# Softmax shifts of one column each, and an addition of zeros for the copy of the bias columns

## What is computed

```python
def _cross_attention(q_in, kv_in, wq, bq, wk, bk, wv, bv, wo, bo, bias_k, bias_v):
    qh = (q_in @ wq + bq).reshape(b, q_len, H, K)
    kh = (kv_in @ wk + bk).reshape(b, t, H, K)
    vh = (kv_in @ wv + bv).reshape(b, t, H, K)
    kh = jnp.concatenate([kh, jnp.broadcast_to(bias_k, (b, 1, H, K))], axis=1)
    vh = jnp.concatenate([vh, jnp.broadcast_to(bias_v, (b, 1, H, K))], axis=1)
    logits = jnp.einsum('bqhk,bthk->bhqt', qh, kh) / scale
    weights = jax.nn.softmax(logits, axis=-1)
    ctx = jnp.einsum('bhqt,bthk->bqhk', weights, vh).reshape(b, q_len, H * K)
    return ctx @ wo + bo
...
x = res + _cross_attention(_layer_norm(x, ...), xf, ...)     # twice
h = jax.nn.gelu(_layer_norm(x, ...) @ w_fc1 + b_fc1, approximate=False) @ w_fc2 + b_fc2
return x + h
```

## Time and profile before

| | |
|---|---|
| median of 3 runs | 567.76 us (566.6 to 568.83) |
| span of the profiled execution | 565.1 us |
| PE busy | 548.0 us (97%) |
| PEld busy | 492.8 us (87%) |
| DVE busy | 408.8 us (72%) |
| ACT busy | 315.1 us (56%) |
| POOL busy | 330.1 us (58%) |
| chain that ended last | PE 82%, DVE 11%, issue 3%, DMA 1%, ACT 1% |

### The profile page before, as it was taken

One profiled execution on the slowest core, in us unless ns is written; L12 is line 12 of the kernel. 1 busy time (PEld: TensorE's weight loads), 2 busy tenths in 40 slices (PEclk: granted clock), 3 DMA queues, 4 the chain that ended last, 5 costly groups with the idle time before them and its releaser, 6 DMA issues.

```text
span 565.1 us, 11067 instructions
## 1 busy us (share of the span) xinstructions
PE 548.0 (97%) x3665; PEld 492.8 (87%) x3665; DVE 408.8 (72%) x802; ACT 315.1 (56%) x707; POOL 330.1 (58%) x380
## 2 busy tenths in 40 slices
PE   7999999999999999999899999999999999999887
PEld 5979899898989899898879989898998989897787
DVE  3995776858586776858787685958768685858884
ACT  3475564747475564737266473746556474756432
POOL 3765655738364664837947393646557383746730
PEclk8999999999999999999999999999999999999999
DMA  7403030302102030301203020120203020000101
GB/s 240 128 22 73 19 74 0 78 15 56 37 22 70 18 75 0 74 20 54 77 19 94 1 74 19 43 50 19 74 0 92 1 71 22 0 19 2 38 1 38
DMA packets 26398, 25.85 MB, mean 46 GB/s; under 512 B 1530, under 2 KB 26254, under 8 KB 26382
## 3 DMA queue, kind: packets, MB, share of 16 engines
q1 hardware_dynamic: 26382, 25.64, 16.8%
HBM read 25.11 MB, written 0.52 MB: 45 GB/s over the span
## 4 chain that ended last, share of the span: by engine, by line
PE 82%; DVE 11%; issue 3%; DMA 1%; ACT 1%; POOL 0%; SPq 0%; DVEq 0%; ACTq 0%; POOLq 0%
PE ring L855 44%; PE ps_ctx L855 20%; PE acc L855 10%; PE ring L893 8%; DVE row_max L634 5%; DVE shift L640 2%; DMA probs<-ctx_in 1%; DVE z_sb L681 1%; ACT probs L469 1%; DVE x_sb L662 1%; DVE k_hi L841 0%; DVE cols L729 0%; DVE h_full L688 0%; DVE bn L670 0%; PE ring L930 0%
## 5 line engine op out<-in xcount | busy, mean ns | idle before, releaser
L336 POOL TENSOR_TENSOR v_lo<-v_sum,v_hi 128x512 fp32r<-128x512 f32 x64 | 82.2, 1295 | 129.1 <-ACT v_hi L448 127.3
L343 POOL TENSOR_SCALAR probs<-probs,inv 128x512 f32<-128x512 f32 x128 | 87.2, 694 | 63.9 <-DVE inv L656 63.9
L469 ACT ACTIVATE probs<-ring,shift 128x512 f32<-128x512 f32 x113 | 77.4, 685 | 32.3 <-DVE shift L640 28.7
L634 DVE TENSOR_REDUCE row_max<-ring 128x1 f32<-128x512 f32 x113 | 75.9, 685 | 11.6 <-PE ring L855 11.6
L448 ACT ACTIVATE v_hi<-v_sum 128x512 fp32r<-128x512 f32 x64 | 40.4, 632 | 77.4 <-DVE v_sum L611 77.4
L618 DVE TENSOR_TENSOR pT_lo<-ring,pT_hi 128x512 fp32r<-128x512 f32 x126 | 81.2, 684 | 3.0 <-ACT pT_hi L455 0.5
L455 ACT ACTIVATE pT_hi<-ring 128x512 fp32r<-128x512 f32 x126 | 69.9, 594 | 0.6 <-PE ring L893 0.5
L855 PE MATMUL ps_ctx<-pT_lo,v_hi 128*128 128x256 f32 x236 | 67.6, 286 | 0.0
L893 PE MATMUL ring<-ident,probs 128*128 128x128 f32 x504 | 65.8, 273 | 1.0 <-POOL probs L343 0.7
L855 PE MATMUL ps_ctx<-pT_hi,v_lo 128*128 128x256 f32 x236 | 66.1, 280 | 0.0
L855 PE MATMUL ps_ctx<-pT_hi,v_hi 128*128 128x256 f32 x236 | 66.1, 280 | 0.0
(11 more groups left out here) (153 smaller groups left out, 1537.3 us busy)
## 6 DMA issues: line engine op xcount, KB each, us to landing
wk_raw<-wk_in SPq DMA_DIRECT2D x17, 256.0 KB, 2.8
wv_raw<-wv_in SPq DMA_DIRECT2D x16, 256.0 KB, 2.7
vrows<-vrows_in SPq DMA_DIRECT2D x16, 256.0 KB, 4.8
wq_raw<-wq_in SPq DMA_DIRECT2D x16, 256.0 KB, 2.6
wo_raw<-wo_in SPq DMA_DIRECT2D x16, 256.0 KB, 2.7
wf_raw<-wf_in SPq DMA_DIRECT2D x7, 256.0 KB, 2.7
probs<-ctx_in SPq DMA_DIRECT2D x2, 512.0 KB, 5.2
x_sb<-x_in SPq DMA_DIRECT2D x1, 512.0 KB, 7.1
```

Source lines behind the costliest of these rows:

```text
L336: pool.tensor_tensor(v_lo[:, 2 * m:2 * m + 2, :], v_sum[:, m % 2, :].rearrange("p (t c) -> p t c", c=PW), v_hi[:, 2 * m:2 * m + 2, :].bitc ...
L343: pool.tensor_scalar(probs[:, u, q, :], probs[:, u, q, :], inv[:, u, q:q + 1], 0.0, ALU.mult, ALU.add).then_inc(p_ready, 1)
L469: act.activation(probs[:, u, q, :], ring[S_BANKS[where][QTB * u + q]][:], ACT.Exp, bias=shift[:, u, q:q + 1], scale=SCALE, accum_out=row_s ...
L634: dve.reduce_max(row_max[:, u, q:q + 1], ring[S_BANKS[where][QTB * u + q]][:], AX_X).then_inc(max_done, 1)
```

## The change

In DVE's program `shifts`, which handled the columns of one or two tiles in one instruction, becomes `shift_of`, which handles one column and counts the semaphore `shift_ready` up by one, and `shifts`, which calls it for both tiles. In units 1 to 3 that makes two instructions where there was one, behind both maxima as before; unit 0 keeps its instructions. `copy_cols` becomes an addition of the six columns and a tile of zeros, `no_cols`, which GpSimd clears among its first instructions.

```diff
@@
         cols = sb("cols", [P, 3, 2])
+        no_cols = sb("no_cols", [P, 6])
@@
             pool.memset(minus_half[:], -0.5)
+            pool.memset(no_cols[:], 0.0)
@@
-            def shifts(pair, u, tiles=range(QTB)):
-
-                part = slice(tiles[0], tiles[-1] + 1)
-                dve.wait_ge(max_done, NS * pair + QTB * u + tiles[-1] + 1)
-                dve.tensor_scalar(shift[:, u, part], row_max[:, u, part], -SCALE, 0.0, ALU.mult, ALU.min).then_inc(shift_ready, len(tiles))
+            def shift_of(pair, u, q):
+
+                dve.wait_ge(max_done, NS * pair + QTB * u + q + 1)
+                dve.tensor_scalar(shift[:, u, q:q + 1], row_max[:, u, q:q + 1], -SCALE, 0.0, ALU.mult, ALU.min).then_inc(shift_ready, 1)
+
+            def shifts(pair, u):
+                for q in range(QTB):
+                    shift_of(pair, u, q)
@@
                     if u == 0:
-                        shifts(pair, u, range(q, q + 1))
+                        shift_of(pair, u, q)
@@
-                dve.tensor_copy(cols[:].rearrange("p g h -> p (g h)"),
-                                step_cols[:, bass.ds(pair + 1, 1), :, :].rearrange("p n g h -> p (n g h)"))
+                dve.tensor_tensor(cols[:].rearrange("p g h -> p (g h)"),
+                                  step_cols[:, bass.ds(pair + 1, 1), :, :].rearrange("p n g h -> p (n g h)"), no_cols[:], ALU.add)
```

## The result

The changed kernel took 562.65 us in the median of 6 runs (560.48 to 563.82); the kernel before, run beside it, 568.24 (566.6 to 569.02). The ratio is 0.9906, with a 95% interval of 0.9888 to 0.9924: by that ratio 5.3 us less (4.3 to 6.4). Forecast were 562.8 us and 5.0 less.

The account below looks back on a forecast made before the run. PE bounds the kernel, busy 548.0 of 565.1 us, so only its waits, traced to two-column shifts held by GpSimd, can be won. Loop 4.9 plus last pair 0.1 gives 5.0: 567.8 to 562.8 us, range 559.8 to 566.4.

Parts of the forecast that it names:

- One column isn't held: Shifts of units 1 to 3: a one-column shift doesn't wait for GpSimd's instruction and takes 0.15 us (bounds 0.15 and 1.08).
- ACT is late next: Unit 2: its exponential then waits for ACT, 0.58 us behind `k_hi`, starting at 99.46 instead of 99.71.
- 0.25: Unit 2, each of 12 loop steps: us that PE regains once the exponential no longer waits for the shift.
- 0.38: Us PE loses per loop step from `scores(3, 0)` to `project_q(0)`: 1.54 against 1.16 in pair 0.
- Sum 0.41 a step: Loop steps: gains at units 2 and 3 added, 0.41 us a step, x12 = 4.9 us.
- 0.16: Unit 3: us PE loses per step in `project_k(2)` and `(3)`, 2.92 against 2.76, all taken as regained.
- `total` takes over the wait: Units 1 and 2: `total`, adding two SBUF tiles, is held by GpSimd instead, to about 99.67 and 104.19.
- What follows keeps its place: VectorE and GpSimd work behind `total` stays on time; `o_lo` of unit 0 ends 0.09 us before `context(1)` wants it.
- rival B: The wait returns to PE through `o_lo`: the 0.16 is lost, 3.0 us stays, 564.8 us; chance 14%.
- The addition brings nothing: Addition replacing the column copy: held by GpSimd as the copy was, no gain; bounds nothing and 0.5 us each in pairs 0, 8.
- Pair 7 and the last pair: Outside the loop steps: pair 7 ends on VectorE's chain, gain nothing; the last pair's split shift gains 0.1 us (0 to 0.3).
- Rival D: `total` of unit 3 comes behind `wo_lo`, `o_lo` 1.20 us late a step; 577.3 us in all 12; chance 3%.

Follow-up runs that it names:

- The first run: Kernel before with the shifts of units 1 to 3 as one column each, the copy of the columns kept: 562.14 us against 567.78, ratio 0.9897.
- the runs with one unit each: Kernel before with the two-column shift split in unit 2 only: 566.82 us, ratio 0.9987; in unit 3 only: 566.27 us, ratio 0.9974.
- the last run: Changed kernel with `total` as two one-column scalar additions and the bias columns copied by ACT instead of VectorE's addition: 561.34 us against 567.66, ratio 0.9883.
- two runs: GpSimd's `wq_lo` and `wv_lo` in the steps shortened to two columns: on the kernel before 565.38 us, ratio 0.9955; on the changed kernel 564.85, ratio 0.9948.

## Why the prediction was right

- *One column isn't held:* right, on one stretch of the trace. The first run confirms it for all 128: 150 ns in the mean; in the changed kernel the longest takes 156.
- *ACT is late next:* right in size. 0.25 of the 0.38 was to come back, and 0.23 did: the matmuls in question now take 1.31 us (98.13 to 99.44), where the earlier trace rows have 1.54 and 1.16.
- *Sum 0.41 a step:* measured 0.41 in the step shown and 0.39 in the mean, 4.7 us in twelve for 4.9. But it stood as a sum of two terms, 0.25 and 0.16, and the runs with one unit each show 0.05 and 0.14. The reading of two separate losses, each with its own price, is the step that was wrong. The 0.16 holds by itself; the 0.25 is there only behind it. The sum came out right because the change removed both, and a forecast for unit 2 alone would have been 3.0 us, where its run shows 0.7 by the ratio, and 1.6 at the end of the interval.
- *`total` takes over the wait:* right, with VectorE's busy time unchanged. "What follows keeps its place" was off: from the start of the step (91.91, now 90.25) `o_lo` of unit 0 ended after 15.30 us and now after 15.08. Its margin is 0.31 us (105.33 against the load one matmul before 105.87), not 0.09, and so rival B had less for it than the 14% it got.
- *The addition brings nothing:* right, 12.7 us in the run where the copy had 12.8, and no difference in time with it alone. In pairs 0 and 8 the bound of 0.5 was too high; the last run shows 0.3.
- *Pair 7 and the last pair:* the first, forecast at nothing, gave 0.16 us (23.50 to 23.34 from its start to the first new rows of `x_sb`); the last 0.13, forecast at 0.1.
- *Rival D:* its mechanism is real, as two runs show, though not in this kernel. Its price of 1.20 us a step was too high: there `wo_lo` itself ran earlier, and PE lost 0.23 (the twelve matmuls of `context(1)` at 1.64 instead of 1.41).

## What to carry to other kernels

A small VectorE instruction that takes far longer than its size asks is to be compared with GpSimd's instruction at the same time: when both end together, it was held, and what matters is who waits for it. Put the hold where nobody waits, rather than removing it; and before pricing several waits of one loop one by one, ask whether each is reached earlier once the one ahead of it is gone. A change of GpSimd's schedule alone, even one that only takes work away, can move such a hold to a place where it costs.

## What the runs showed of the hardware that I had not expected

- Three columns in one scalar operation are held like two (0.82 us beside `wq_lo`), one column is not (0.15), nor is one column with a second operand read from SBUF (0.21).
- Padding two tiles of 32 bytes a partition to 48 made the matmuls of `context` and `output` 2 to 4 ns slower each, 1.5 us in the run. One operand of each (`pT`, `o`) lies behind the padded tiles, the other (`v`, `wo`) ahead of them. Which distance or alignment does it was not tried.
- Shortening two GpSimd instructions a step by 1.1 us each made the changed kernel 2 us slower.
